# The last five steps of a fused attention and expert kernel, written out in an order of their own

## The reference, cut to what matters

```
att = jnp.einsum('bthd,btgd->bthg', q, k) / np.sqrt(HD)
att = jax.nn.softmax(att, axis=-1)
out = jnp.einsum('bthg,btgd->bthd', att, v).reshape(b, t, D)
x = x + (out @ Wo + bo)
...
gate = jax.nn.softmax(h2 @ Wg + bg, axis=-1)
combined = jnp.einsum('btd,edf,bte->btf', h2, We, gate)
```

## Time and profile before

| | us |
|---|---|
| median of 3 runs | 276.04 (275.45 to 277.45) |
| the profiled execution, its own time | 274.52 |
| its span, first to last instruction | 272.5 |
| TensorE matmul busy | 240.0 (88%) |
| VectorE busy | 193.0 (71%) |
| ScalarE busy | 169.7 (62%) |
| GpSimd busy | 163.9 (60%) |

### The profile page before, as it was taken

How to read it: one execution, slowest core, us unless ns; L and a number is a source line. 1 busy time by engine, 2 the same in 40 slices (tenths; PEclk the granted TensorE clock), 3 DMA queues, 4 the chain that set the end, 5 groups by cost and what they waited for, 6 DMA issues and landing times.

```text
span 272.5 us, 7694 instructions
## 1 busy us (share of the span) xinstructions
PE 240.0 (88%) x3146; PEld 169.4 (62%) x3146; DVE 193.0 (71%) x327; ACT 169.7 (62%) x502; POOL 163.9 (60%) x173
## 2 busy tenths in 40 slices
PE   7999979897999999999999999899999797843770
PEld 6765766767676675859585867586857374612320
DVE  0237543479798888888889714998889988998710
ACT  3546516483868768777776767657786555744431
POOL 4104042546476777868684538656877777898544
PEclk9999999999999999999999999999999889996555
DMA  6990000000000000000000000000000000000000
GB/s 196 362 301 9 0 4 2 4 0 5 0 2 10 2 13 4 10 2 12 4 2 10 2 11 2 12 2 0 5 10 2 12 5 11 2 10 10 0 10 10
DMA packets 6016, 7.28 MB, mean 27 GB/s; under 512 B 477, under 2 KB 4830, under 8 KB 5982
## 3 DMA queue, kind: packets, MB, share of 16 engines
q1 hardware_dynamic: 5550, 6.16, 7.1%
q10 hardware_dynamic: 432, 0.64, 0.7%
HBM read 5.88 MB, written 0.92 MB: 25 GB/s over the span
## 4 chain that ended last, share of the span: by engine, by line
PE 65%; ACT 13%; DVE 13%; issue 4%; POOL 2%; DMA 1%; POOLq 0%; SPq 0%; ACTq 0%; DVEq 0%
PE ps_a L658 36%; PE ps_c L658 12%; PE ps_b L658 8%; DVE ps_e L529 5%; ACT probs L359 5%; PE ps_b L710 3%; PE ps_e L658 3%; DVE psums L497 2%; DVE ps_e L554 2%; ACT exb L414 2%; DMA cT<-in_ctx_t 1%; ACT junk L398 1%; ACT qT L342 1%; POOL exb L281 1%; DVE prod L543 1%
## 5 line engine op out<-in xcount | busy, mean ns | idle before, releaser
L261 POOL TENSOR_TENSOR prod<-fqkv 128x1280 f32<-128x1280 f32 x14 | 40.7, 2906 | 3.4 <-DVE fqkv L515 1.9
L658 PE MATMUL ps_c<-fwe_sb,x2T 128*128 128x512 f32 x56 | 34.4, 710 | 5.6 <-DVE glog L571 5.6
L252 POOL TENSOR_TENSOR probs<-probs,prinv 120x672 f32<-120x672 f32 x16 | 22.8, 1427 | 23.8 <-DVE prinv L501 23.7
L414 ACT ACTIVATE exb<-ps_c,gate 128x128 f32<-128x128 f32 x112 | 32.5, 397 | 6.4 <-POOL gate L304 4.2
L658 PE MATMUL ps_a<-aT,wo_sb 128*128 128x112 f32 x256 | 32.9, 281 | 1.0 <-issue 0.6
L658 PEld LDWEIGHTS ps_a<-aT,wo_sb 128*128 128x128 f32 x256 | 29.9, 191 | 3.6 <-issue 1.5
L529 DVE TENSOR_REDUCE ps_e<-prod 128x256 f32<-128x2048 f32 x14 | 32.0, 2286 | 0.0
L281 POOL TENSOR_TENSOR exb<-exb 128x640 f32<-128x640 f32 x14 | 21.6, 1540 | 17.3 <-ACT exb L414 17.3
L554 DVE TENSOR_REDUCE ps_e<-prod 128x128 f32<-128x2048 f32 x14 | 31.3, 2239 | 0.0
L658 PE MATMUL ps_a<-wv_sb,cT 128*64 128x512 f32 x128 | 31.0, 605 | 0.0
L271 POOL TENSOR_TENSOR prod<-e_sb,fqkv 128x768 f32<-128x768 f32 x14 | 25.3, 1810 | 7.2 <-ACT e_sb L387 7.2
(11 more groups left out here) (122 smaller groups left out, 456.8 us busy)
## 6 DMA issues: line engine op xcount, KB each, us to landing
xp_sb<-in_xp SPq DMA_DIRECT2D x1, 896.0 KB, 8.0
out<-out_sb SPq DMA_DIRECT2D x14, 64.0 KB, 1.5
xT<-in_x_t SPq DMA_DIRECT2D x1, 784.0 KB, 9.5
cT<-in_ctx_t SPq DMA_DIRECT2D x1, 784.0 KB, 11.1
wv_sb<-in_wv SPq DMA_DIRECT2D x1, 512.0 KB, 8.0
wo_sb<-in_wo SPq DMA_DIRECT2D x1, 512.0 KB, 12.2
fwe_sb<-in_fwe SPq DMA_DIRECT2D x1, 512.0 KB, 9.0
fw_sb<-in_fw SPq DMA_DIRECT2D x1, 266.0 KB, 11.7
```

The lines of the kernel that those rows point to most:

```text
L252: nc.gpsimd.tensor_tensor(pr[0:TG, NC:C, :, 0:S], pr[0:TG, NC:C, :, 0:S], prinv[p % 2][0:TG, NC:C, :].unsqueeze(3).to_broadcast([TG, C - N ...
L261: nc.gpsimd.tensor_tensor(prod1[:, 0:HP, :, :], t[:, D:2 * D].rearrange("p (g d) -> p g d", g=FH).unsqueeze(1).to_broadcast([128, HP, FH, ...
L414: last = nc.scalar.activation(exb[f % XB][:, e, :], ps_c[:, half, e % 4 * D:(e % 4 + 1) * D], ACT.Copy, scale=gate[f % 2][:, e:e + 1])
L658: return nc.tensor.matmul(o, lhsT, rhs, start=start, stop=stop, skip_group_check=True)
```

## The change

- Steps 2 to 13 keep their loop, with some calls moved. ScalarE: `squares` and `x2_copy` go behind the projection's copies and stand ahead of `x1_copy`; `head_exps` comes ahead of the first `values`; `kv_copy` ahead of the experts. VectorE: `logits` goes ahead of `new_x2`, `prob_sums` and `norm`; the reciprocal of the sums is split from `mixed_heads` as `head_scales`, ahead of `gate_sum`. GpSimd: `norm` ahead of `second_scale`. TensorE: the bias product of `new_o` is a part of its own, `bias_o`, ahead of `shift`.
- Steps 14 and 15 have an own loop on each engine. Both halves of the experts come ahead of `attend`; the gate logits come ahead of `shifted_logits` on VectorE; `scaled_qkv` ahead of `weighted`.
- What was steps 16 to 19 is a list without steps, for the tiles `third` (11), `prior` (12) and `last` (13). The head products of tile 13 stand ahead of the head sums of tile 12 on VectorE.
- For tiles 10 to 13 GpSimd makes 8 and 5 heads of the products in place of 10 and 6; VectorE makes 8 and 11 in place of 6 and 10.
- The experts of tiles 11, 12 and 13 go to `ps_b`, `ps_a` and `ps_b`. Their products wait for `x2T` and for the former users of the banks, no more for the gate logits.
- Tile 13: its gate is computed on VectorE; four experts are multiplied and added by VectorE straight from the accumulator (`last_experts`) while ScalarE copies the other four; `last_residual` on GpSimd adds the two residual terms first; VectorE makes the last three additions (`last_sums`).
- `stay_warm`: ten products of 128 columns on the identity, which nothing reads, between the gate logits of tile 12 and the bias product of tile 13.
- The seven products at the start become one of 512 columns.

```
-            for _n in range(WARM_UP):
-                nc.tensor.matmul(ps_b[:, 0, 0:128], ident[:, :], ident[:, :], start=True, stop=True)
+            nc.tensor.matmul(ps_b[:, 0, :], ident[:, :], ident[:, :].unsqueeze(1).to_broadcast([128, 4, 128]), start=True, stop=True)
...
+def product_heads(f):
+    return (HP_LATE, HQ_LATE) if f >= LATE else (HP, HQ)     # LATE = 10, HP_LATE = 8, HQ_LATE = 5
...
 scalar, steps 2 to 13
                 if t < NP:
                     exps(t)
-                if fc is not None:
-                    squares(fc)
                 for fill in PROJECT_AT.get(t, ()):
                     project(*fill)
+                if fc is not None:
+                    squares(fc)
+                    x2_copy(fc)
                 if fa is not None:
                     x1_copy(fa)
-                if fc is not None:
-                    x2_copy(fc)
-                if t < NP:
-                    values(t, 0)
                 if fb is not None:
                     head_exps(fb)
                 if t < NP:
+                    values(t, 0)
                     values(t, 1)
                     turned_probs(t)
...
 vector, after step 15
+            products(prior)
+            new_x1(NP - 1)
+            logits(prior)
+            new_x2(third)
+            shifted_logits(prior)
+            scaled_qkv(last)
+            weighted(prior)
+            products(last)
+            head_sums(prior)
+            head_scales(prior)
+            gate_logits(third)
+            normed_heads(prior)
+            logits(last)
+            gate_sum(third)
+            shifted_logits(last)
+            new_x2(prior)
+            weighted(last)
+            head_scales(last)
+            head_sums(last)
+            gate_logits(prior)
+            normed_heads(last)
+            gate_sum(prior)
+            new_x2(last)
+            gate_logits(last)
+            gate_sum(last)
+            last_gating(last)
+            last_experts(last)
+            last_sums(last)
...
 tensor, after step 15
+            new_y(NP - 1)
+            turn_o(third)
+            bias_o(third)
+            new_o(third)
+            first(last)
+            turn_x2(third)
+            gate_logits(third)
+            turn_o(prior)
+            expert_half(third, 1)
+            bias_o(prior)
+            new_o(prior)
+            expert_half(third, 0)
+            turn_x2(prior)
+            expert_half(prior, 0)
+            gate_logits(prior)
+            stay_warm(prior)
+            bias_o(last)
+            turn_o(last)
+            expert_half(prior, 1)
+            new_o(last)
+            turn_x2(last)
+            gate_logits(last)
+            expert_half(last, 1)
+            expert_half(last, 0)
...
+            def stay_warm(f):
+                pe.wait_ge(s["onorm_ready"], f + 1)
+                for _n in range(STAY_WARM):
+                    mm(ps_e[:, f % 2, 0:128], ident[:, :], ident[:, :])
...
+            def last_experts(f):
+                x = exb[f % XB]
+                dve.wait_ge(s["last_base"], 1)
+                dve.wait_ge(s["gate_ready"], f + 1)
+                dve.wait_ge(s["hi_made"], f + 1)
+                for e in range(4, E):
+                    if e > 4:
+                        dve.wait_ge(s["last_acc"], e - 4)
+                    nc.vector.scalar_tensor_tensor(out=x[:, E, :], in0=expert_banks(f)[:, 1, (e - 4) * D:(e - 3) * D], scalar=gate[f % 2][:, e:e + 1],
+                                                   in1=x[:, E, :], op0=ALU.mult, op1=ALU.add).then_inc(s["last_acc"], 1)
```

More of the change, by code:

```diff
@@ L326, in _ @@
                     gating(fc)
+            for t in range(TAIL, END):
+                fa, fb, fc, fd = (TILE_AT.get(t - k) for k in range(4))
+                products(fb)
+                outputs(fd)
+                norm(t)
+                second_scale(fc)
+                first_scale(fa)
+                weighted(fb)
+                gating(fc)
+            last, prior, third = NT - 1, NT - 2, NT - 3
+            products(prior)
+            first_scale(last)
+            weighted(prior)
+            products(last)
+            second_scale(third)
+            outputs(third - 1)
+            gating(third)
+            weighted(last)
+            second_scale(prior)
+            outputs(third)
+            gating(prior)
+            second_scale(last)
+            last_residual(last)
+            outputs(prior)
         @block.scalar
@@ L473, in _ @@
                 if fc is not None:
+                    experts(fc, 0)
                     experts(fc, 1)
+            for t in range(TAIL, END):
+                fa, fb, fc = (TILE_AT.get(t - k) for k in range(3))
+                o_copy(fc)
+                exps(t)
+                x2_copy(fc)
+                squares(fc)
+                x1_copy(fa)
+                turned_probs(t)
+                values(t, 0)
+                head_exps(fb)
+                values(t, 1)
+                gate_exps(fc)
+                attended(t, 0)
+                attended(t, 1)
+                kv_copy(fa)
+                experts(fc, 1)
+                experts(fc, 0)
+            last, prior, third = NT - 1, NT - 2, NT - 3
+            o_copy(third)
+            x1_copy(last)
+            head_exps(prior)
+            x2_copy(third)
+            squares(third)
+            kv_copy(last)
+            gate_exps(third)
+            o_copy(prior)
+            head_exps(last)
+            squares(prior)
+            experts(third, 1)
+            experts(third, 0)
+            x2_copy(prior)
+            gate_exps(prior)
+            o_copy(last)
+            experts(prior, 1)
+            x2_copy(last)
+            squares(last)
+            experts(prior, 0)
+            gate_exps(last)
+            experts(last, 0)
         @block.vector
@@ L630, in _ @@
                     new_x1(t - 1)
+                if fb is not None:
+                    logits(fb)
                 if fc is not None:
@@ L820, in _ @@
             attend(1)
-            for t in range(2, LAST_STEP + 1):
+            for t in range(2, TAIL):
                 fa, fc = TILE_AT.get(t), TILE_AT.get(t - 2)
@@ L857, in _ @@
                     expert_half(fc, 1)
+            for t in range(TAIL, END):
+                fa, fb, fc = TILE_AT.get(t), TILE_AT.get(t - 1), TILE_AT.get(t - 2)
+                scores(t)
+                new_y(t - 1)
+                turn_o(fc)
+                shift(t)
+                bias_o(fc)
+                new_o(fc)
+                first(fa)
+                turn_x2(fc)
+                values(t, 0)
+                gate_logits(fc)
+                values(t, 1)
+                turn_probs(t)
+                expert_half(fc, 1)
+                expert_half(fc, 0)
+                attend(t)
+            last, prior, third = NT - 1, NT - 2, NT - 3
+            new_y(NP - 1)
[22 more added lines that the diff above has]
+            expert_half(last, 0)
 def kernel(**inputs):
```

141 lines of the change are left out of this document (107 added, 34 removed).

## The result

The kernel after takes 265.39 us (median of 4 executions, 264.92 to 266.37), against 275.75 for the kernel before in the same comparison: ratio 0.9625, interval 0.9584 to 0.9666. It is faster, as forecast, but by about 4 us more than forecast. The profiled execution took 265.66 us, its span is 263.8 us, and the mean granted clock over the span 0.977 (before 0.947).

A forecast was written before the change was run, and what follows sets the result against it. Prediction: TensorE bounds up to 206 us, VectorE to 257, then a chain of waits. Terms -2.0 - 6.15 + 1.5 = -6.65 us gave span 265.9, median near 269.4; 8-in-10 range 267.0 to 273.5.

The forecast's parts named there:

- Steps 2 to 13, forecast -2.0: Main loop: moving squares and putting logits earlier shorten TensorE's waits, 2.0 us gained, bounds 0 to 2.2.
- the 0.35 and 0.30 written: Steps 3 and 11: gains in us from exponentials coming about 1 us sooner, so TensorE's 0.98 us wait shrinks.
- E: Slower rival, steps 4 to 13: late logits delay head_exps and attend waits; 278.4 us at 1.2 us delay; chance 0.07.
- 0.12 us in each of the 9 steps ... and no more: Projection in steps with squares: moving it behind the copies cuts 3.58 to 3.46 us, 1.1 us in all.
- The start, forecast +1.5: First projection: with one warm-up product about half its records run at half clock, 1.5 us lost through to the end.
- Rival C: The start costs nothing, its 16 records still at full clock: 267.9 us; chance 0.10.
- From step 14 to the last head softmax, forecast -2.3: VectorE-bound stretch: waits and gaps removed, less 1.6 us for extra heads; onorm of tile 13 comes 2.3 us sooner.
- The last tile, forecast -3.85: From onorm of tile 13 to the end: shorter chain of additions, copies and gate, less added costs; 3.85 us gained.
- The +0.4 for the order of the transfers: Last tile: tile 12's output ends with tile 13's and its transfer is issued first, costing 0.4 us.
- The dummies, forecast +1.5 at the turn: Last tile: ten dummy products at full clock, with the bias product behind them, delay tile 13's turn by 1.5 us.
- Rival B: Dummies run at half clock, up to 4.3 us, moving the end by 2.1 us: 271.5 us; chance 0.20.
- From the span to the median, forecast +3.5: Whole run: span 265.9 us, profiled execution near 267.9, median near 269.4, using the kernel before's differences.

The follow-up runs named there:

- The loop alone: Kernel before with only the new order of steps 2 to 13; start, steps 14 to 19 and last tile as before: 271.49 us, ratio 0.9882.
- The start alone: Kernel before with one warm-up product of 512 columns in place of the seven at the start: 274.67 us, ratio 0.9977.
- the old split: Kernel after with GpSimd again making 10 and 6 heads of the products for tiles 10 to 13: 266.7 us, ratio 0.9663.
- the gate edit: Kernel after with the exponentials of tile 13's gate written to accumulator memory (PSUM) in place of SBUF: 266.86 us, ratio 0.9667.

## Why the prediction was too high

- **Steps 2 to 13, forecast -2.0: right in kind, too small.** Each term named is there: the fillings are shorter, the waits of steps 3 and 11 went from 0.98 to 0.69 us, near the 0.35 and 0.30 written, step 12's is gone, and no step waits longer for the turned probabilities (E did not come). The mis-sized term is "0.12 us in each of the 9 steps ... and no more". It measured 0.25 to 0.26 (3.58 to 3.33). I had read 3.46 in two steps without `squares` as the floor; these steps also lack the tile's `new_o` between the maxima and the projection, so the exponentials hold up the copies, and they take 3.46 us in the kernel after still. The loop alone measured 3.2 us.
- **The start, forecast +1.5 "carried on in full, as TensorE is the bound from there": the step that failed.** The loss was there (1.9 us); the carrying on was not. The stream already contained 2.19 us of stalls of TensorE's own issue, which I had in no term, and they stand at fixed counts of records. With six products fewer, slower records lie ahead of record 470, and the largest stall shrank from 1.37 us to between 0 and 0.47. The start alone: 0.9977 [0.9941, 1.0014]. Rival C gave the right price by luck: its reason was that the first 16 records would still run at full clock, and they took 5.38 us.
- **From step 14 to the last head softmax, forecast -2.3, measured -3.0.** The waits went as listed, to 0.69 us in total against 0.6 forecast. The mis-sized term is VectorE's work. I had 1.6 us more of it, for the heads; from the row maxima of pair 14 on, its busy time rose by 0.5 us only (43.91 to 44.43), while its idle time fell from 4.91 to 1.36. The heads themselves cost 1.3 us of busy time (43.17 with the old split), and in the profile waits of the same size went with them; where the other 0.7 us of busy time went is not shown.
- **The last tile, forecast -3.85, measured -2.9.** The gate on VectorE was to be cheaper and cost 1.13 us for 0.29: the meeting with GpSimd that I feared for the additions fell on the gate, and took 0.85 us more. The Trainium skill ("SBUF — State Buffer", the section on the two separate sides) gives the condition for that too: besides two SBUF inputs it names VectorE's two-port modes, and the loser blocks until the other has ended. The trace agrees for the gate (both end within 0.03 us), and so does the edit that moves the operand out of SBUF; in which mode the gate ran, no trace shows. In the additions, where I had applied it, the first (128x256) took 0.61 us beside GpSimd's last, 0.2 more than its 0.42 in the trace of the gate edit, and the others (128x128) 0.29: a price of 0.2 us, where I had 0.3 to 0.4. The +0.4 for the order of the transfers was nothing.
- **The dummies, forecast +1.5 at the turn, measured 1.7.** They ran at full clock in the execution profiled (2.48 us for 2.2), and the other three executions have the same mean granted clock, 0.977. Rival B, dummies at half clock, did not come in this kernel as far as that tells, but it did in the profiles of two others with the same ten products (4.11 and 4.41 us). That they gain something I did not forecast, and the runs show no gain.
- **From the span to the median, forecast +3.5, measured +1.6.** I added the distance of the median of three executions from the profiled one. Up to 1.0 us of these 1.9 is that sample's height; the rest is where single profiled executions lie: the kernel before's was low, the kernel after's is in the middle of its four.

Together: 2.3 us at the first stretch, 0.7 at the second, -0.95 at the third, and 1.9 from the baseline give the 4.0 us between 269.4 and 265.4. My range took in costs of the clock and the queue, but had no case in which the start was free and the gain of the fillings twice its stated size. The 270.7 given as the upper bound of the terms is no sum of them (the start's 3.2 us alone gives 271.1); nothing hung on it. My outer bound for the start, "nothing", was the right end of it.

**Open.** Whether the issue stalls are waits for instructions. The counts of records and the transfers speak for it in all 13 traces, but the trace does not say which engine a transfer serves, and no experiment separated the number of products from the time of arrival. That the steps from pair 5 on take up most of what is left is seen in the table, not explained. A version clearly better than the kernel after was not found: the split of the heads, the dummies' number and place, the gate's operand and the last transfer all lie within 1.5 us of it.

## What to carry to other kernels

Before a loss at the start is carried through a stream bound by one engine, count that engine's idle time by reason. For stalls that aren't waits for data, count the records ahead of them in several kernels too: here they stood at the same counts whatever the kernel and the time, so that adding or taking out instructions far ahead changed which work lay in front of them, and with it their length. Take the floor of an operation from the shortest row of its form in the whole trace (3.33 us stood there once, at 27 us) and not from steps that differ in more than the neighbour in question. For a late small VectorE operation look at what GpSimd runs at that moment, and keep its operand in PSUM if the two would meet.

## What the runs showed of the hardware

- TensorE's issue stalls, 38 rows of 0.2 to 1.65 us in 13 traces, all stand behind 470, 845, 1220, 1594, 2594 or 2968 to 2969 matmul records, and a transfer of 16 KB of instructions starts 2.2 to 2.8 us before each ends. The first took 1.37 us in the kernel before, and 0.47 us with the short start, 12 records further on in the program.
- A VectorE operation on 8 values a partition took 1.13 us beside a GpSimd addition and 0.29 with its tensor operand in PSUM.
- The granted clock of TensorE in the last 15 us differs between executions of nearly the same stream: two expert records at about 250 us took 1.12 or 1.13 us in six kernels' profiles and 2.08 in two. The executions of one kernel lie 1.0 to 4.5 us apart, and the clock makes at most part of this: the four of the kernel after all have a mean clock of 0.977 and lie 1.4 us apart; without the dummies the two slowest of six have 0.957 and 0.964, the others 0.971 to 0.974.
- While TensorE was at half clock in that stretch, VectorE's way from `onorm` of tile 12 to that of tile 13 took 9.4 us instead of 8.4, in the two profiles where it stayed there.
